# A Mamba and mixture-of-experts block: the order of small steps around the router and of one low part

## What is computed

```python
h = tok(x)                              # 16 images x 64 patches = 1024 tokens of width 192
h = h + attn(layernorm(h))
h = h + ffn(layernorm(h))
# attn, the selective scan over the 64 tokens of an image, 384 channels, 16 states:
dt  = softplus(ts @ dt_proj + b)        # last token's dt times alpha
dA  = exp(A * dt);  dBu = dt * B * h
state = dA * state + dBu;  y = sum_n(state * C)
y = (y + h * D) * silu(gate)            # last token's y times feature_gating
# ffn, 8 experts of hidden size 512, the two best of a token, and a shared one:
scores = softmax(x @ gate_w.T);  w, idx = top_k(scores, 2);  w = w / sum(w)
y = sum_e cw[:, e] * (silu(x @ w1[e].T) * (x @ w3[e].T)) @ w2[e].T  +  shared(x)
```

## Time and profile before

| | us |
|---|---|
| median of 3 runs | 372.35 (372.12 to 372.91) |
| the profiled execution's own time | 372.61 |
| its span, first to last instruction | 370.8 |
| TensorE busy | 328.7 (89%) |
| VectorE busy | 251.2 (68%) |
| GpSimd busy | 204.9 (55%) |
| ScalarE busy | 194.1 (52%) |

### The profile page before, as it was taken

One profiled execution on the slowest core, in us unless ns is written; L12 is line 12 of the kernel. 1 busy time (PEld: TensorE's weight loads), 2 busy tenths in 40 slices (PEclk: granted clock), 3 DMA queues, 4 the chain that ended last, 5 costly groups with the idle time before them and its releaser, 6 DMA issues.

```text
span 370.8 us, 6616 instructions
## 1 busy us (share of the span) xinstructions
PE 328.7 (89%) x2034; PEld 263.8 (71%) x2035; DVE 251.2 (68%) x475; ACT 194.1 (52%) x332; POOL 204.9 (55%) x162
## 2 busy tenths in 40 slices
PE   5799977989998788799788879899999999999990
PEld 5753855747875676588675568678888888888870
DVE  1455799979998999999998699883333333333330
ACT  1146895937995666676925757752222222222220
POOL 8110088695896999898866258600333333333342
PEclk9899899989999999999899989999999999999998
DMA  6990899200023320410999992232333222333222
GB/s 189 261 322 6 332 320 334 61 1 5 0 99 129 115 113 4 113 44 2 233 240 302 272 241 92 101 93 56 46 53 51 48 44 48 50 50 50 36 21 21
DMA packets 32776, 42.60 MB, mean 115 GB/s; under 512 B 3328, under 2 KB 28720, under 8 KB 31728
## 3 DMA queue, kind: packets, MB, share of 16 engines
q1 hardware_dynamic: 26752, 36.43, 33.9%
q0 software_dynamic: 4080, 4.39, 7.6%
q10 hardware_dynamic: 1920, 1.46, 1.7%
HBM read 28.29 MB, written 13.99 MB: 114 GB/s over the span
## 4 chain that ended last, share of the span: by engine, by line
PE 58%; DVE 18%; issue 10%; ACT 7%; DMA 4%; POOL 1%; SPq 1%; DVEq 0%; POOLq 0%; ACTq 0%
PE ps L1977 9%; DVE decays L1208 6%; PE ps L1803 6%; PE ps L1757 4%; PE ps L1935 4%; PE ps L1941 3%; PE ps L1940 3%; PE ps L1936 3%; PE ps L1937 3%; PE ps L1938 3%; DMA c_all<-in_xT 3%; PE ps L1967 3%; DVE w L424 3%; ACT decays L861 2%; PE ps L1566 2%
## 5 line engine op out<-in xcount | busy, mean ns | idle before, releaser
L623 POOL TENSOR_TENSOR states<-decays,c_all 128x1024 f32<-128x1024 f32 x48 | 113.9, 2401 | 18.1 <-DVE decays L1208 18.1
L1208 DVE TENSOR_TENSOR_SCAN decays<-decays,ps 128x1024 f32<-128x1024 f32 x48 | 107.4, 2262 | 4.6 <-PE ps L1757 4.0
L729 POOL DMA_INDIRECT out<-ysb,token_r x23 | 36.1, 1570 | 69.5 <-DVE ysb L1467 58.0
L861 ACT ACTIVATE decays<-dt,negA 128x504 f32<-128x504 f32 (+1 forms) x104 | 62.0, 675 | 8.1 <-POOL states L623 8.0
L981 ACT ACTIVATE sa<-ps 128x512 f32<-128x512 f32 x31 | 18.5, 598 | 87.6 <-PE ps L1941 85.5
L1803 PE MATMUL ps<-ident,states 128*128 128x128 f32 x384 | 54.1, 285 | 3.4 <-POOL states L623 1.9
L1977 PE MATMUL ps<-w,hT 128*128 (+1 forms) x248 | 46.3, 330 | 3.8 <-ACT hT L985 3.8
L1757 PE MATMUL ps<-diagB,stacked_u 64*128 64x128 f32 x384 | 38.1, 295 | 12.0 <-DVE decays L1208 10.4
L1803 PEld LDWEIGHTS ps<-ident,states 128*128 128x128 f32 x384 | 42.5, 144 | 7.6 <-POOL states L623 2.9
L1977 PEld LDWEIGHTS ps<-w,hT 128*128 128x128 f32 x248 | 42.0, 191 | 7.2 <-ACT hT L985 3.7
L1757 PEld LDWEIGHTS ps<-diagB,stacked_u 64*128 64x128 f32 x384 | 28.4, 188 | 25.4 <-DVE decays L1208 15.5
(11 more groups left out here) (217 smaller groups left out, 595.1 us busy)
## 6 DMA issues: line engine op xcount, KB each, us to landing
rows_scratch<-zeros SPq DMA_DIRECT2D x16, 520.0 KB, 9.5
c_all<-c_scratch SPq DMA_DIRECT2D x8, 1024.0 KB, 4.7
w_raw<-in_w13T SPq DMA_DIRECT2D x9, 512.0 KB, 9.7
w_raw<-in_w13T SPq DMA_DIRECT2D x18, 256.0 KB, 9.6
w<-in_w2T SPq DMA_DIRECT2D x9, 384.0 KB, 3.2
xs<-rows_scratch SPq DMA_DIRECT2D x23, 130.0 KB
c_all<-in_xT SPq DMA_DIRECT2D x8, 256.0 KB, 9.1
out<-h SPq DMA_DIRECT2D x1, 576.0 KB, 3.3
```

The lines of the kernel that those rows point to most:

```text
L623: pool.tensor_tensor(states[:, n % SLOTS, :].rearrange("p (n b s) -> p n b s", n=NH, b=2), decays[:, k % DBUF, t, :, :, :].rearrange("p b ...
L729: pool.indirect_dma_start(out=out_d, out_offset=bass.IndirectOffsetOnAxis(ap=token_r[:, r:r + 1], axis=0), in_=ysb[:, r, :], in_offset=Non ...
L861: return act.activation(decays[:, k % DBUF, tiles[0]:tiles[1], :, n, 1:], dt[g][:, i, tokens].rearrange("p (a b s) -> p a b s", b=2, s=S)[ ...
L1208: dve.tensor_tensor_scan(both, both, unit_banks(n).rearrange("p b n -> p (b n)"), 0.0, ALU.mult, ALU.add).then_inc(scan_ok, 1)
```

## The change

The edits are in two places. In the scans `u_low_part(3)` moves on VectorE from behind scan 20 to behind scan 21, `time_step(1, 2)` from behind scan 21 to behind scan 22, and GpSimd's `inputs_of(1, 1)` and `(1, 2)` from behind products 21 and 23 to behind 22 and 24. In the tail:

- ScalarE does high part 6 ahead of the copies of pair x, does the first exponent directly behind the table load, then high parts 7 and 8, `h_copy(1)`, high part 9, and only then the second exponent. `CONVERTED` is 10, so high parts 10 and 11 stand behind step 1, and so on, two earlier than before.
- VectorE does `token_weights(0)` and `slots(0)` ahead of `logits_out(1)`.
- TensorE turns the second logits (`logits_by_token(1)`) behind the first half of up(2), not ahead of it.
- `tile_experts` is cut in two: its last seven operations (`tile_rows`) come one step later.

```diff
-        FIRST_STEP, CONVERTED = 1, 8
+        FIRST_STEP, CONVERTED = 1, 10
...
-                if n in (18, 21, 23):
-                    inputs_of(pool, 1, (18, 21, 23).index(n))
+                if n in (18, 22, 24):
+                    inputs_of(pool, 1, (18, 22, 24).index(n))
...
             silu(1, 1)
+            high_part(act, 6)
             for p in range(2):
                 act.wait_ge(xn_tr, G + 2 + p)
                 out, x = pair_x(p)
                 act.activation(out, x, ACT.Copy).then_inc(tail_x[p], 1)
             h_copy(0, 0)
-            act.preload_act_table_set("natural_log_exp_and_others")
-            high_part(act, 6)
-            for g in range(G):
+            def exponents(g):
+
                 act.wait_ge(lmax_ok, g + 1)
                 tiles = slice(TPG * g, TPG * (g + 1))
                 act.activation(sc[:, tiles, :], lg[:, tiles, :], ACT.Exp).then_inc(lexp_ok, 1)
-                if g == 0:
-                    high_part(act, 7)
+
+            act.preload_act_table_set("natural_log_exp_and_others")
+            exponents(0)
+            high_part(act, 7)
+            high_part(act, 8)
+            h_copy(1, 1)
+            high_part(act, 9)
+            exponents(1)
             act.wait_ge(tail_x[1], 1)
 
-            stage_loop(act, [(1, silu), (0, h_copy), (2, x_high)], TILES - 1, behind)
+            def next_h_copy(s, r):
+                if not isinstance(s, int) or s > 1:
+                    h_copy(s, r)
+
+            stage_loop(act, [(1, silu), (0, next_h_copy), (2, x_high)], TILES - 1, behind)
...
-                if n == 20:
+                if n == 21:
                     u_low_part(3)
-                if n in (17, 20, 21):
-                    time_step(1, (17, 20, 21).index(n))
+                if n in (17, 20, 22):
+                    time_step(1, (17, 20, 22).index(n))
...
                 chain(dve.tensor_tensor(tcmp[:, :, :], tcmp[:, :, :], ends, ALU.mult))
+
+            def tile_rows():
+
                 chain(dve.tensor_reduce(first_tile[:, :], tcmp[:, :, :], AX.X, ALU.max))
...
                 if s == 2:
                     tile_experts()
+                if s == 3:
+                    tile_rows()
...
             result(0, 0)
-            logits_out(1)
             token_weights(0)
             slots(0)
+            logits_out(1)
             read_logits(1)
...
                 up_first(s, r, we)
+                if isinstance(s, int) and s == 2:
+                    logits_by_token(1)
                 h_transposes(s - 1, 1 - r)
...
             ranks(0)
-            logits_by_token(1)
```

## The result

On one chip and in alternation the kernel before took a median of 372.11 us (367.78 to 373.85, 20 executions) and the changed kernel 370.22 us (366.05 to 373.88, 20 executions). The ratio of the two is 0.992 with a 95% interval of 0.9895 to 0.9945. The ratio leaves out executions more than 1.5% above the fastest of their kernel, 6 of the 20 of the changed kernel and 2 of the 20 of the kernel before, and says 3.0 us where the medians of all, and the means of all, say 1.9. With the later comparisons of this study there are 44 executions of the changed kernel and 130 of the kernel before: means 369.54 and 371.98, a difference of **2.45 us (plus or minus 0.70)**; the three sets of executions that hold both kernels give 1.9, 2.8 and 2.5 one by one. The forecast was 2.3 us.

A forecast was written before the change was run, and what follows sets the result against it. VectorE was taken to bound the scans and shared stages, TensorE the routed stages. Scans 1.5 plus tail 0.8 made 2.3 us off the median of 372.35, so 370.1 us, with a range of 369.2 to 371.9.

The forecast's parts named there:

- Scans, 1.5 us: Scans: VectorE's 1.79 us wait behind scan 20 goes, the first time step costs slightly more; 1.5 us gained.
- the 0.1 that I took off for GpSimd: Scans: 1.6 us earlier at scan 24 was taken as 1.5 for the scans, with GpSimd's product 28 ending 1.0 to 1.3 earlier.
- Rivals A: Scans: GpSimd's product 22 starts ahead of the second time step, 2.3 us lost; gain 0.1, time 372.2; chance 0.10.
- C: Scans: GpSimd becomes the bound through its two moved uses and only the tail's gain stays; 371.5 us; chance 0.05.
- B: Tail: it gives nothing, leaving only the 1.5 us of the scans; 370.9 us; chance 0.18.
- h copy and exponent, nothing: Tail: TensorE's wait of 2.33 us ahead of down(1) moves to up(3), about 3.0 us long; no gain.
- Slots ahead of the second logits: Tail: weights and slots done before the second logits; VectorE reads the turned logits 0.15 us later.
- Table in two steps: Tail: seven table operations move one stage on; up(5) starts near 232.8 instead of 234.18, half given back at up(6).
- the tail in sum, 0.8: Tail: VectorE's waits less 0.15 us for the later logits give 0.87, taken as 0.8 at routed stage 8.
- What it can gain is its waits, 0.48 + 0.21 + 0.33: Tail: VectorE's work is unchanged, so its gain can only come from its three short waits, 1.02 us together.
- Rival D, the clock: Tail, up(3): 1.2 GHz through two stages behind the longer wait gives 375.0 us; one 3.4 us stretch hidden; chance 0.05.

The follow-up runs named there:

- e2: The kernel before with the tail edits alone, its scans unchanged; median 371.15 us, ratio to before 1.000.
- e6: The changed kernel with ScalarE's old order of the tail (h copy and conversions behind the exponents); median 370.57 us, ratio to before 0.998.
- e1: The kernel before with the scan edits alone, its tail unchanged; median 370.98 us, ratio to before 0.998.
- e5: The changed kernel with the second step of the tile table one stage later, behind step 4; median 369.12 us, ratio to before 0.991.
- e16: The changed kernel again, unaltered, in the last job; median 368.88 us, ratio to before 0.993.
- e12: The kernel before with TensorE's transposes and 10 idle products ahead of scan unit 34; median 370.44 us, ratio to before 0.991.
- e13: The kernel before with the scan edits alone, plus transposes and 10 idle products ahead of scan unit 34; median 368.57 us, ratio to before 0.992.
- e8: The changed kernel again, unaltered, in the second job; median 368.89 us, ratio to before 0.991.
- e9: The changed kernel with TensorE's transposes of the sixth chunk of u moved ahead of scan unit 34's inputs; median 369.44 us, ratio to before 0.988.
- e4: The changed kernel with the table of tiles in one step as before; median 371.23 us, ratio to before 0.998.
- e3: The changed kernel with 16 idle products on TensorE ahead of up(3); median 369.04 us, ratio to before 0.995.
- e7: The changed kernel with 16 idle products ahead of up(3) and 10 ahead of scan unit 34, values changed; median 368.13 us, ratio to before 0.990.
- e10: The changed kernel with transposes and 10 idle products ahead of scan unit 34 and 16 ahead of up(3); median 367.88 us, ratio to before 0.990.
- e11: The changed kernel with ScalarE's old tail order, transposes and 10 idle products ahead of scan unit 34; median 368.40 us, ratio to before 0.986.
- e15: The changed kernel with both waits filled (scan unit 34 and up(3)), once more; median 367.86 us, ratio to before 0.992.
- e14: The kernel before with transposes and 10 idle products ahead of scan unit 34, once more; median 370.07 us, ratio to before 0.996.

## Why the prediction was right or wrong

**Scans, 1.5 us: right, a little low.** The wait of 1.79 went, the first step cost 1.35 against the 1.29 to 1.44 worked out, the second 0.66, and scan 24 came 1.71 us earlier. Nothing was lost behind it: 86.84 - 85.14 = 1.70 was still there at up(0), so the 0.1 that I took off for GpSimd was not needed. Rivals A and C did not come, nor, at the high clock, did B: it would leave the tail at 50.87, and e2 has 50.33. The race that A is about went the same way in every profile with the scan edits, the second step at 0.66.

**h copy and exponent, nothing: right.** The wait moved to up(3) and is 3.01 us as said; e6 undoes the edit and keeps 50.30.

**Slots ahead of the second logits: nearly.** VectorE read the turned logits at 212.77, 17.39 us behind up(0) against 215.28 - 198.07 = 17.21 before: 0.18 later, forecast 0.15.

**Table in two steps, and the tail in sum, 0.8: right in kind, too large.** At the high clock the tail gives 0.54. Of the three waits, the 0.48 (result of stage 4) and the 0.21 are gone; but the result of stage 5, which waited 0.33 before (0.61 in e1), still waits 0.49 in e2 and 0.50 in the changed profile. up(5) came 36.01 - 34.54 = 1.47 us earlier behind up(0) (e1 against e2; forecast 1.4), and up(6) 40.49 - 40.01 = 0.48: two thirds of it given back, not half. The step that failed in the tail is "What it can gain is its waits, 0.48 + 0.21 + 0.33": the sum took all three for 0.8, the tail gave 0.54, and the last one stayed, since TensorE had lost most of its lead again by then.

**Rival D, the clock: dismissed by a wrong step.** I wrote that one stretch of 3.4 us is hidden, that the sign is decided "from about 9 us at the low level", and against it that "the trace has no low stretch of that length in the tail". One trace was taken for all, and what lies between 3.4 and 9 us was put at nothing in the sum, though the prediction's own terms price it: half of 6.8 us less the lead of 2.0 is 1.4, and 1.3 was measured. Even 3.4 us are hidden only in part: they cost 0.1 (before), 0.2 (e5, e16), 0.5 and 0.6 us (e12 with 51.37, e13 with 51.51, both in the old order of 50.87), by where they fall. And 6.8 us are not hidden, they cost 1.3, and in that length they came in three of seven profiles with the unsplit wait of 3.0 us (the first, e8, e9), 3.4 us in three more (e4, e5, e16); only e2 had none. In the six profiles where that wait is filled or split (e3, e6, e7, e10, e11, e15) only e11 shows low clock there. The old order, with its wait of 2.33 us ahead of down(1), is between the two: 3.4 us in three of five profiles (before, e12, e13), 6.8 in none. The Trainium skill ("TensorE: Matmul & The Clock Gate", section on HAM oscillation) describes a kernel in which TensorE's wait ahead of every tile brings the low clock back, each time anew. The counts here agree in part, with waits of 1.9 and 3.0 us: the low level came behind most of them and not behind each. It did not turn the sign, since the stretch cost less than the change gains, but it took 1.3 us of 2.2 in the profile that was shown.

**The range: the step that failed.** 370.1 lies 0.1 from the median of the changed kernel and the gain of 2.3 is inside 2.45 +- 0.70. The ratio of 0.992, times 372.11, gives 369.1, 0.1 below the low end of 369.2. The step is "The range runs from 369.2 (both upper bounds and a little more)": it was made from the bounds of the terms, each known to some tenths, and the spread of executions with the clock was put at nothing beyond that little. What the runs show in its place: the 20 executions of the changed kernel run from 366.05 to 373.88, low time accounts for 80% of such variance, and a mean over 20 is known to about a microsecond; the same 40 executions give 1.9 or 3.0 us by the way of averaging. That, and not a term of the sum, put the result outside. The errors of the terms found above (scans 0.2 too low, tail 0.26 too high) nearly cancel, so that 2.3 meets the 2.2 of the profiles at equal clock owes something to luck; and a result 0.1 beyond or inside the low end is within the noise in any case.

**What stays open.** If all executions are brought to equal low time with the slope of 0.33, the change gains 3.3 +- 0.5 us, 1.1 more than the profiles account for; with the waits filled (e10 and e15 against e12 and e14) it is 1.6, so the excess is not in every pairing. A part of this is that the slope prices the change's additional low time, 24.0 against 21.5 us, too high: its first 3.4 us behind unit 34 cost 0.15 per us (0.5 for 3.4), and those in the tail 0.2 (1.3 for 6.8). That part is 2.5 x (0.33 - 0.17) = 0.4. The rest is not settled. Nor is it settled that the change itself raises the low time: the two intervals touch, and where both kernels' clocks are known from one job (e8 and e16 beside the kernel before) it is 22.7 +- 2.5 against 21.0 +- 1.3. The kernel before gained from the fill at unit 34 too (1.4 +- 1.1 us), though neither of its two unfilled scan profiles showed the stretch; why is open.

## What to carry to other kernels

A wait on the bounding engine that names a late producer was worth nearly its full length here (1.71 of 1.79 us), since something of equal price could be done in it, and the new place could be costed to 0.1 us from rows of the same kernel; in a crowded part behind it, count only those waits whose producer really comes earlier. A wait of another engine that is hidden by its length can still cost through what follows it: look up TensorE's granted clock behind each of its waits, compare profiles at equal clock, and price a low stretch by how far TensorE's lead carries it. Idle matmuls in such a wait are cheap to try: they took the low stretch away here, though what that saves was within the noise. And when single executions spread over 2%, the range of a forecast needs a share for that, beside the bounds of its terms.

## What the runs showed of the hardware

The granted clock fell in stretches of 3.4 or 6.8 us (3.42, 6.84; beside them only the one at the very end of each profile), at places that differ between executions of one kernel: e8 and e16 are the same program, and one has none and the other 6.8 us behind unit 34. The first 110 us of the kernel, untouched by any of these edits, took 108.1 to 113.0 us in the profiles. A wait of TensorE of 1.9 us in the scans was followed by one in 6 of 8 profiles, one of 3.0 us in the tail in 6 of 7; in both places some stretches began inside the wait. Those that did lasted 6.8 us, five of five (the first profile, e8 and e9 in the tail, e4 and e16 at unit 34), and those that began when TensorE was back at work lasted 3.4, seven of eight (e4, e5, e16 in the tail, e1, e3, e5 and e6, with its first matmul, at unit 34; e9's at unit 34 lasted 6.8). Filled with products, neither wait had a low stretch in or behind it: five profiles at unit 34 with the scan edits, and four in the tail (e3, e7, e10, e15). The price of a VectorE step with two SBUF inputs beside GpSimd's products repeated to a few hundredths: 1.33 to 1.36 us at the new place in all profiles with the scan edits, 1.18 to 1.20 at the old one, and 0.66 where it started ahead of the product, which then took 2.75 instead of 2.38.
